# A graph layer and an expert layer on one core: TensorE makes the Clifford product behind the degrees, VectorE compares before it makes the gate sums

## The reference

```python
h   = layernorm(x)                                   # 6250 x 256
hc, rc = to_hypercomplex(h), to_hypercomplex(rel)    # 4 blades x 64
gate = sigmoid(rc[type] @ gate_w.T + gate_b)         # one number for each relation
m   = clifford_linear(hc[src] * rc[type], msg_w, msg_b) * gate
deg_src, deg_dst = counts of each node in src, in dst
m   = m * max(deg_src[src] * deg_dst[dst], 1) ** -0.5
agg = segment_sum(m, dst)
x   = x + clifford_linear(hc + agg, upd_w, upd_b)
# then, on layernorm(x): a router's softmax over 8 experts, each of three 256 x 256
# layers (two with batch norm and relu), their outputs weighted and added to x
```

## Time and profile before

| | |
|---|---|
| median of 3 runs | 1969.09 us |
| the profiled execution: time | 1968.35 us |
| its span | 1966.5 us |
| PE, PEld busy | 95%, 86% |
| DVE, ACT, POOL busy | 40%, 51%, 71% |
| mean granted TensorE clock | 0.959 of 2.4 GHz |

### The profile page before, as it was taken

The page is one execution under the profiler, slowest core; times in us unless marked ns, Lnnn a source line. Parts: engine busy times, 40 slices in busy tenths (PEclk is TensorE's granted clock), DMA queues, the critical chain, the costliest instruction groups (busy, mean ns, idle before and its releaser), DMA issues.

```text
span 1966.5 us, 35243 instructions
## 1 busy us (share of the span) xinstructions
PE 1867.5 (95%) x13045; PEld 1689.2 (86%) x13046; DVE 787.6 (40%) x1833; ACT 1005.1 (51%) x2286; POOL 1405.1 (71%) x1410
## 2 busy tenths in 40 slices
PE   5837978999999999999999999999999999999998
PEld 4827977989989989988998998998998998998888
DVE  6964333343333433334334333343343333343342
ACT  3734644555545545545555455555555554553445
POOL 3867777777777777777777777777777777777600
PEclk8557989999999999999999999999999999999999
DMA  8166434434434434434434434444443443443400
GB/s 242 52 223 213 125 106 121 125 103 125 124 104 125 126 102 124 124 103 127 123 104 125 124 107 121 126 113 115 125 124 102 127 124 103 126 111 106 105 12 6
DMA packets 97137, 232.32 MB, mean 118 GB/s; under 512 B 24748, under 2 KB 45482, under 8 KB 97055
## 3 DMA queue, kind: packets, MB, share of 16 engines
q0 software_dynamic: 66336, 184.06, 35.1%
q1 hardware_dynamic: 29904, 46.21, 7.5%
q10 hardware_dynamic: 815, 1.16, 0.2%
HBM read 217.90 MB, written 13.44 MB: 118 GB/s over the span
## 4 chain that ended last, share of the span: by engine, by line
PE 86%; POOL 6%; issue 3%; DVE 3%; DMA 0%; ACT 0%; SPq 0%; DVEq 0%; POOLq 0%
PE z L750 33%; PE y L780 17%; PE agg L795 16%; PE pr L804 9%; POOL H L404 4%; PE y L726 3%; PE y L717 2%; POOL R L404 2%; PE y L678 2%; DVE H L933 2%; PE z L702 1%; PE y L738 1%; PE y L718 1%; PE y L772 1%; DVE big L973 0%
## 5 line engine op out<-in xcount | busy, mean ns | idle before, releaser
L404 POOL DMA_INDIRECT H<-h_table,src x784 | 768.3, 980 | 246.8 <-issue 244.7
L404 POOL DMA_INDIRECT R<-r_table,typ x598 | 624.4, 1044 | 201.3 <-issue 199.8
L588 ACT ACTIVATE h<-z,bns 128x256 f32<-128x256 f32 (+1 forms) x864 | 416.6, 539 | 622.1 <-PE z L750 619.5
L1137 DVE SCALAR_TENSOR_TENSOR acc<-y,wg,acc 128x256 f32<-128x256 f32 x392 | 173.5, 480 | 679.8 <-PE y L780 679.5
L795 PE MATMUL agg<-S,H 128*86 128x64 f32 x4704 | 396.3, 242 | 0.7 <-issue 0.7
L795 PEld LDWEIGHTS agg<-S,H 128*86 128x86 f32 x4704 | 392.3, 159 | 1.9 <-issue 1.2
L750 PE MATMUL z<-hT,big 128*128 128x256 f32 (+1 forms) x1728 | 384.8, 366 | 1.9 <-ACT h L588 1.9
L780 PE MATMUL y<-big,h 128*128 128x256 f32 x1568 | 378.2, 382 | 1.7 <-DVE lg L1100 1.6
L750 PE MATMUL z<-h,big 128*128 128x256 f32 (+1 forms) x1728 | 375.9, 360 | 0.4
L750 PEld LDWEIGHTS z<-h,big 128*128 128x128 f32 x1728 | 305.3, 191 | 36.8 <-ACT h L588 1.0
L780 PEld LDWEIGHTS y<-big,h 128*128 128x128 f32 x1568 | 291.3, 190 | 42.1 <-issue 1.9
(11 more groups left out here) (161 smaller groups left out, 1070.3 us busy)
## 6 DMA issues: line engine op xcount, KB each, us to landing
H<-h_table,src POOLq DMA_INDIRECT x784, 2.8
tb<-in_typ_row SPq DMA_DIRECT2D x24, 448.0 KB
R<-r_table,typ POOLq DMA_INDIRECT x598, 2.8
h_table<-big SPq DMA_DIRECT2D x7, 910.0 KB
big<-in_x SPq DMA_DIRECT2D x7, 896.0 KB, 10.9
big<-in_w SPq DMA_DIRECT2D x8, 768.0 KB, 4.5
acc<-in_x SPq DMA_DIRECT2D x22, 256.0 KB, 5.4
out<-acc SPq DMA_DIRECT2D x22, 256.0 KB
```

The source lines that it names most:

```text
L404: pool.indirect_dma_start(out=to[:, b * DX:(b + 1) * DX], out_offset=None, in_=tab, in_offset=bass.IndirectOffsetOnAxis(ap=ix[:, J * SB + ...
L588: last = s_.activation(o[:, m, 0:wide_], z_[:, m, 0:wide_], ACT.Relu, bias=bns[:, l, 1, c:c + 1], scale=bns[:, l, 0, c:c + 1])
L1137: last = v.scalar_tensor_tensor(out=acc[:, g % 3, t, :], in0=b[:, t * D:(t + 1) * D], scalar=wg[:, t, e_:e_ + 1], in1=acc[:, g % 3, t, :], ...
```

## The change

TensorE's program has the Clifford product behind the degree loop. VectorE fills `orow` and `lrow` before the indices have come, makes the first round of one-hots directly behind the casts, then the gate sums, then the second round. ScalarE sums the first chunk of x before it waits for the gate sums, and the second chunk before it waits for the sigmoids.

```diff
@@ scalar
+                early = min(2, XS // XN)
+
                 def sums_of(c):
...
+                sums_of(0)
                 act.wait_ge(gsum, 1)
                 s_.activation(egate[0:RT, :], gate[0:RT, :], ACT.Exp, scale=-1.0).then_inc(gexp, 1)
-                sums_of(0)
+                for c in range(1, early):
+                    sums_of(c)
                 act.wait_ge(gated, 1)
                 act.wait_ge(z_row, 1)
...
-                for c in range(1, XS // XN):
+                for c in range(early, XS // XN):
                     sums_of(c)
@@ tensor
-                pe.wait_ge(cl_ready, 1 + 2 * len(NEG))
-                for m in range(3):
-                    for k in range(2):
-                        last = pe.matmul(AGG[0:M3, m, 0:D], km[:, k, m * M3:(m + 1) * M3], UT[:, k, :],
-                                         start=k == 0, stop=k == 1)
-                last.then_inc(w2_mm, 1)
                 pe.wait_ge(oh_done, 1)
                 with pe.Fori(0, HIT) as i:
...
+                pe.wait_ge(cl_ready, 1 + 2 * len(NEG))
+                for m in range(3):
+                    for k in range(2):
+                        last = pe.matmul(AGG[0:M3, m, 0:D], km[:, k, m * M3:(m + 1) * M3], UT[:, k, :],
+                                         start=k == 0, stop=k == 1)
+                last.then_inc(w2_mm, 1)
                 pe.wait_ge(consts, 2)
@@ vector
                 v.tensor_copy(iota_cb, iota_w[:, 0:P].unsqueeze(2).to_broadcast([P, P, HB]))
+                for g in range(NG):
+                    if END[g] > BEGIN[g]:
+                        v.memset(orow[:, BEGIN[g]:END[g]], float(origin[g]))
+                        v.memset(lrow[:, BEGIN[g]:END[g]], float(span[g] - W))
                 dve.wait_ge(ld_src, 16)
...
                 v.tensor_copy(hi_b, hi_i).then_inc(bins, 1)
-                dve.wait_ge(ld_rel, 48)
-                link(v.tensor_tensor(rprod[0:RT, :, :], rel[0:RT, :, :], gwb[0:RT, 0:D].unsqueeze(1).to_broadcast([RT, 4, D]), ALU.mult))
-                link(v.reduce_sum(gate[0:RT, :], rprod[0:RT, :, :], AX.X))
-                v.tensor_scalar(gate[0:RT, :], gate[0:RT, :], gbc[0:RT, :], None, ALU.add).then_inc(gsum, 1)
                 dve.wait_ge(bins, 1)
                 dve.sem_inc(oh_used, 2)
...
                 first = min(2, HIT - 1)
-                onehots(0, first)
+                onehots(0, first // 2)
+                dve.wait_ge(ld_rel, 48)
+                link(v.tensor_tensor(rprod[0:RT, :, :], rel[0:RT, :, :], gwb[0:RT, 0:D].unsqueeze(1).to_broadcast([RT, 4, D]), ALU.mult))
+                link(v.reduce_sum(gate[0:RT, :], rprod[0:RT, :, :], AX.X))
+                v.tensor_scalar(gate[0:RT, :], gate[0:RT, :], gbc[0:RT, :], None, ALU.add).then_inc(gsum, 1)
+                onehots(first // 2, first)
                 dve.wait_ge(gexp, 1)
...
-                for g in range(NG):
-                    if END[g] > BEGIN[g]:
-                        v.memset(orow[:, BEGIN[g]:END[g]], float(origin[g]))
-                        v.memset(lrow[:, BEGIN[g]:END[g]], float(span[g] - W))
                 dve.wait_ge(dloc_done, 1)
```

## The result

| | before | after |
|---|---|---|
| median | 1968.59 us (1967.8 to 1969.21, 4 runs) | 1956.57 us (1956.1 to 1958.35, 4 runs) |
| span of the profiled execution | 1966.5 us | 1954.7 us |
| mean granted TensorE clock | 0.959 | 0.980 |
| first gather from `h_table` | 141.34 us | 129.56 us |

The ratio is 0.9941, with a 95% interval of 0.9924 to 0.9958: faster by 12 us. I had forecast 1957 us, a span of 1954.7 us and the gather at 129.5 us.

A forecast was written before the change was run, and what follows sets the result against it. The part after GpSimd's first gather from `h_table` was taken to hang on that gather; 12.3 us earlier minus 0.5 us lost gave -11.8 us, from 1968.35 to 1956.6, stated as 1957 us, range 1953 to 1962.

The forecast's parts named there:

- the main part: The stretch behind GpSimd's first gather from `h_table`, said to hang on that gather, forecast at 129.5 us instead of 141.34.
- The loop can't be sped up by order, only started earlier: Degree loop of VectorE and TensorE over two buffers: 5.77 us a round, both engines nearly full.
- The first round at 8.80 us: VectorE's first one-hots start behind the casts: casts end at 8.61 us, plus 0.19 for the loop's entry.
- The gate sums, the second round, the sigmoids: VectorE's next steps, ending at 16.99, 22.62 and 23.12 us, so the fifth half starts 12.3 us earlier.
- ScalarE.: ScalarE's early sums are in time for the sigmoids; store of `r_table` issued about 25.2 us, landing at 31.5.
- Gathers from `r_table` end near 124 us: GpSimd's 45 gathers, 2.78 us each beside one-hots, still end some 4 us before `h_table` lands.
- 0.5 us for more gathers beside the store of `h_table`: Loss from about 2 us more of gathers beside that store on full DMA engines: between 0 and 1.3 us.
- The Clifford product costs nothing behind the degrees: TensorE's 12 matmuls of 4.27 us, moved to about 98 us, end by 107, before the 114 us reader.
- upper bound of 8.5 us: Longest time allowed for the moved Clifford product on TensorE, at the granted 0.50 clock (1.2 GHz).
- The memsets, nothing: 54 memsets taken from VectorE's check, 0.93 us, off the path: nothing counted, at most 0.9 us of gain.
- The rival of a faster loop: Degree loop: rounds of 5.44 us instead of 5.77 if the clock stays up, 4 us more gain, 1953; chance 0.07.
- the record of 0.50: TensorE's granted clock from 49 to 98 us, the degree loop; the prediction followed it against the skill's rule.

The follow-up runs named there:

- e2: The changed kernel with the Clifford product put back ahead of the degree loop: 1965.74 us against 1969.09 us, ratio 0.9986.
- e1: The kernel before with the Clifford product moved behind the degree loop and nothing else: 1960.31 us against 1969.09 us, ratio 0.9952.
- e8: The changed kernel with the Clifford product computed five times over behind the degrees: 1959.08 us against 1970.09 us, ratio 0.9947.
- e9: The changed kernel with chunks 1 to 5 of x, in place of chunk 1, summed ahead of ScalarE's sigmoids: 1957.62 us against 1970.09, ratio 0.9936.
- e4: The changed kernel with ScalarE's order of the kernel before (exponentials, chunk 0, store of `r_table`, the other chunks): 1957.44 us, one run.
- e3: The changed kernel with the 54 memsets back in the check: 1956.40 us, one run.
- e10: The changed kernel with the layer-norm statistics of the last 7 tiles on ScalarE in place of VectorE: 1954.99 us against 1970.09, ratio 0.9925.
- e11: The kernel of e10, with SyncE loading the types and first three groups of x only once `r_table` has landed: 1954.37 us against 1970.09, ratio 0.9925.

## Why the prediction was right

The one claim that it rests on is that the main part starts with GpSimd's first gather from `h_table` and keeps its length. Of the ten kernels on undisturbed chips the traces give both numbers:

| | fifth half | first gather from `h_table` | span | rest of the span |
|---|---|---|---|---|
| before | 35.42 | 141.34 | 1966.5 | 1825.2 |
| e2, all but the product | 32.66 | 138.93 | 1962.0 | 1823.1 |
| e1, the product alone | 25.86 | 131.89 | 1959.7 | 1827.8 |
| e8, product five times | 23.18 | 129.82 | 1957.2 | 1827.4 |
| after | 23.16 | 129.56 | 1954.7 | 1825.1 |
| e9, `r_table` late | 23.09 | 129.34 | 1956.7 | 1827.4 |
| e4, ScalarE's old order | 23.38 | 129.79 | 1954.5 | 1824.7 |
| e3, memsets late | 22.90 | 128.86 | 1954.5 | 1825.6 |
| e10, statistics on ScalarE | 24.09 | 127.23 | 1952.7 | 1825.5 |
| e11, types too | 23.07 | 126.37 | 1951.2 | 1824.8 |

While the first gather moves by 15 us the rest stays within 4.7 us, without a trend. The table alone doesn't single out the gather: counted from the check's line 995 or 1000, which moved along in all ten, the rest is 1838.5 to 1843.1 us, as even. What singles it out is the chain of waits up to 345 us: in all ten it runs over the gap ahead of the first gather, where GpSimd waits for `h_table` to land. The scatter of 4.7 us is the real width of such a forecast: the range of 1953 to 1962 us was about right for it, and the hit on 1954.7 us was better than the method is.

Point by point, by the steps of the prediction:

- **The loop can't be sped up by order, only started earlier.** Right: 5.77 us for a round before and after. It could be made shorter by taking other work out of it (e10), which the prediction didn't look for.
- **The first round at 8.80 us.** Measured 8.84, by two errors that cancel, which is luck: the casts ended at 8.18 us, not 8.61, and the way from there to the first compare took 0.66 us, not 0.19. The last cast took 0.56 us for 1.23. GpSimd's cast of the targets lies beside it in both kernels, and the one that starts first keeps its time: before, GpSimd's started at 7.35 us (0.84 us long) and VectorE's at 7.38 (1.23); after, VectorE's at 7.62 (0.56) and GpSimd's at 7.67 (1.20). It is so in all thirteen traces. Of the 0.66 us 0.43 come with the early memsets (0.23 us without them, e3); how they do it no run tells, since they themselves end at 4.09 us, before the indices land.
- **The gate sums, the second round, the sigmoids.** Until 16.99, 22.62, 23.12 us; measured to the next row's start 16.93, 22.55, 23.16. Right.
- **ScalarE.** The sigmoids at 23.1 us and the store of `r_table` issued at 25.2 (measured 24.95). It landed so that the first gather started at 34.09 us, where I had taken 31.5 in a range of 29.9 to 37. The first of two terms that were mis-sized, and e9 shows that it was worth nothing.
- **Gathers from `r_table` end near 124 us.** Measured 123.06, with a gap of 6.50 us (I had said 4 to 5). Still hidden. That the start was 2.6 us later than I had taken and the end still earlier has its reason in a count: 26 gathers of the kernel before were issued until 108.6 us, not 24, since those beside VectorE's statistics take 0.95 us. That is 2.57 us each in place of 2.78; with it, and from 34.09 us on, the gathers end at 123 us.
- **0.5 us for more gathers beside the store of `h_table`.** The second: the shift was 12.26 us at the fifth half, 12.3 at the degrees, and 11.78 at the first gather, so 0.5 us was indeed lost, between the degrees and the gather. But e9 has three more gathers beside the store and lost nothing, and e3, with the change's own gathers, came to 128.86 us. From SyncE's first store to the landing it is 27.08 us before and 27.59 after, 27.09 in e3, 27.47 in e9 and 27.88 in e8. So the 0.5 us are scatter of the landing by all that the runs show; the cause that I had given isn't borne out, and that the sum hit 129.5 us with it is luck.
- **The Clifford product costs nothing behind the degrees.** Right: 4.69 us, and behind it and its matmul (103.4 us) 10.6 us are left until line 1000 reads that (114.0); e8 puts 10.7 us more into that place for 1 to 1.5 us, if for any. My upper bound of 8.5 us had doubled 4.27 us that for the most part were no full-clock time (see the last section).
- **The memsets, nothing.** Right for the time (e3); in e3's trace the fifth half is 0.26 us earlier without them ahead of it; up to 0.9 us better I had allowed for.
- **The rival of a faster loop** fell in a way that I had not thought of: the record of the granted clock did go up to 1.00, and the loop was no faster.

What carries the gain, then, is the product's place (8.8 of 12.0 us alone). TensorE took nothing before a product that is done at 26.6 us and first read at 133.0 (VectorE's copy into `W2T`), and that product waited for GpSimd, which VectorE's own compares held up. VectorE's order gives the other 3 us on top of the move; without the move it gives as much by another way, through GpSimd.

## What to carry to other kernels

Look for the work at the head of an engine's program whose result is needed last: here moving six lines behind a loop of 86 us (TensorE's, 11.7 to 98.0 us) was worth 8.8 us alone. Follow the first instruction that must come early from its data, through every engine that stands ahead of it, and ask for each what it is queued behind. And when two engines fill a loop evenly, look for work of one of them that a third, waiting, engine can take (here 3 us more, to ScalarE, which waited 28).

## What the runs showed of the hardware

**GpSimd is held up by VectorE's compares, both in its own arithmetic and in issuing gathers.** The 64x64 sign flips take 0.36 to 0.49 us with VectorE standing or at its gate sums and 0.89 to 2.04 us beside its bf16 compares of two operands in SBUF (e2 against e1). A gather's issue takes 2.41 to 2.75 us beside them and 0.95 us while VectorE makes layer-norm statistics from one operand (57.5 to 60.8 us). GpSimd in the changed kernel:

```profile
55.96 2.41 POOL L404 DMA_INDIRECT R<-r_table,typ  x1 [0.30 <-issue]
58.67 0.95 POOL L404 DMA_INDIRECT R<-r_table,typ  x1 [0.30 <-issue]
```

The Trainium skill ("SBUF — State Buffer", Who interferes with whom) has the first half of it (a VectorE instruction with two SBUF inputs contends with a GpSimd instruction that reads SBUF); the second half, the gathers, goes against what it infers there.

**The granted clock in the records isn't the pace.** In the degree loop it is 0.50 in the kernel before and in e2, where the Clifford product stands ahead of the loop, and 1.00 in the changed kernel and in e1, where it stands behind. Two halves take 5.46 to 5.54 us in all four, from the third round on. And in the changed kernel, where the record says 1.00, the product that follows the loop starts at the lower pace. TensorE's weight loads in e8, where the record says 1.00 as well:

```profile
98.71 0.27 PEld L682 LDWEIGHTS agg<-UT,H 128*86 128x86 f32 x1 [0.16 <-issue]
99.13 0.27 PEld L682 LDWEIGHTS agg<-UT,H 128*86 128x86 f32 x1 [0.16 <-issue]
...
102.12 3.98 PEld L682 LDWEIGHTS agg<-UT,H 128*86 128x86 f32 x18 [0.16 <-issue]
```

They stand 0.43 us apart, and from 102.1 us on 0.22 us apart: two to one, as 2.4 and 1.2 GHz are. In the changed kernel they stand 0.43 us apart up to 101.7 us. The product at the head of the kernel before shows the same, under a record of 1.00 too:

```profile
24.71 0.27 PEld L670 LDWEIGHTS agg<-UT,H 128*86 128x86 f32 x1 [0.16 <-issue]
25.14 1.18 PEld L670 LDWEIGHTS agg<-UT,H 128*86 128x86 f32 x5 [0.16 <-issue]
```

So I read it that TensorE came out of the loop at its lower clock in both kernels, whatever the record says. The prediction took the record of 0.50 at its word, and it was right for the loop's pace in both. In the four traces the record stands at 1.00 from the start and falls to 0.50 for the first time some microseconds behind the product: between 32 and 33 us in the kernel before, 27 and 28 in e2, 105 and 106 in the changed kernel, 109 and 110 in e1. That would fit a record that shows 1.00 until the first fall behind a real rise; no run here tests it.
